# A TensorE loop over expert tiles, turned by two products

## What is computed

```python
router_logits = x @ gate_w.T
probs = jax.nn.softmax(router_logits, axis=-1)
topw, sel = jax.lax.top_k(probs, 2)
topw = topw / jnp.sum(topw, axis=-1, keepdims=True)
combine = jnp.sum(jax.nn.one_hot(sel, E) * topw[..., None], axis=1)
gu = jnp.einsum('th,efh->etf', x, gate_up_w)      # E = 8, F = 1024, H = 256
gate, up = gu[..., :F], gu[..., F:]
hact = up * jax.nn.gelu(gate, approximate=False)
expert_out = jnp.einsum('etf,ehf->eth', hact, down_w)
out = jnp.einsum('eth,te->th', expert_out, combine)
```

## Time and profile before

| what | value |
|---|---|
| median of three runs | 1316.13 us (1311.7 to 1317.1) |
| span of the profiled execution | 1255.6 us, 60.5 us under the median |
| TensorE (PE) busy | 1159.1 us, 92% of the span |
| DVE, ScalarE, GpSimd busy | 885.0, 570.0, 268.5 us |
| expert part, 338.47 to 931.90 us | 593.4 us, TensorE busy 567.8 |
| whole tiles, half tiles | 28, 11 |
| matmuls of line 1772, of line 1785 | 3744, 1608 |

### The profile page before, as it was taken

How to read it: one execution, slowest core, us unless ns; L and a number is a source line. 1 busy time by engine, 2 the same in 40 slices (tenths; PEclk the granted TensorE clock), 3 DMA queues, 4 the chain that set the end, 5 groups by cost and what they waited for, 6 DMA issues and landing times.

```text
span 1255.6 us, 35065 instructions
## 1 busy us (share of the span) xinstructions
PE 1159.1 (92%) x11816; PEld 968.8 (77%) x11816; DVE 885.0 (70%) x2697; ACT 570.0 (45%) x1187; POOL 268.5 (21%) x394
## 2 busy tenths in 40 slices
PE   4799999998699998999998999999998999999996
PEld 3678888886488887787887888888886777877774
DVE  4688888897376665757656666776566878778773
ACT  4466666675232422424224242422234666666553
POOL 6024444444310000000000000000014344444310
PEclk9899999998799999999999999999998999999998
DMA  9544444445341221222312222100023222322210
GB/s 282 209 131 153 147 149 152 152 142 179 132 157 45 73 96 41 86 63 64 98 39 80 74 67 88 41 31 31 27 65 95 72 78 82 93 88 77 79 39 17
DMA packets 82755, 119.67 MB, mean 95 GB/s; under 512 B 27325, under 2 KB 52557, under 8 KB 80588
## 3 DMA queue, kind: packets, MB, share of 16 engines
q1 hardware_dynamic: 64172, 60.32, 15.4%
q0 software_dynamic: 12848, 49.05, 11.7%
q10 hardware_dynamic: 5616, 8.78, 1.9%
HBM read 63.81 MB, written 47.58 MB: 89 GB/s over the span
## 4 chain that ended last, share of the span: by engine, by line
PE 77%; DVE 9%; issue 6%; ACT 3%; SPq 2%; ACTq 2%; DMA 1%; DVEq 0%; POOL 0%; POOLq 0%
PE bank L1772 27%; PE bank L1785 14%; PE bank L1599 7%; PE bank L1533 6%; PE bank L1455 5%; PE bank L1475 3%; PE bank L1516 3%; PE bank L1586 3%; PE bank L1518 2%; PE bank L1539 2%; PE bank L1597 1%; PE bank L1610 1%; PE bank L1501 1%; PE bank L1559 1%; DVE bm L1093 1%
## 5 line engine op out<-in xcount | busy, mean ns | idle before, releaser
L1772 PE MATMUL bank<-tiles,we 128*128 128x256 f16 (+1 forms) x3744 | 395.1, 259 | 5.8 <-issue 4.9
L1772 PEld LDWEIGHTS bank<-tiles,we 128*128 128x128 f16 x3744 | 325.9, 98 | 47.1 <-issue 13.3
L947 ACT ACTIVATE tiles<-bank 128x256 f32<-128x256 f32 (+1 forms) x312 | 109.5, 354 | 336.3 <-PE bank L1772 300.4
L1785 PE MATMUL bank<-we,tiles 128*128 128x256 f16 x1608 | 225.5, 274 | 20.7 <-DVE tiles L1385 19.8
L1381 DVE SCALAR_TENSOR_TENSOR tiles<-bank,tiles 128x256 f32<-128x256 f32 (+1 forms) x312 | 119.8, 384 | 164.7 <-ACT tiles L947 161.2
L1785 PEld LDWEIGHTS bank<-we,tiles 128*128 128x128 f16 x1608 | 148.1, 98 | 59.3 <-DVE tiles L1385 33.7
L1533 PE MATMUL bank<-qT,kbd 128*128 128x256 f16 x960 | 150.3, 274 | 2.7 <-issue 2.0
L1093 DVE TENSOR_REDUCE bm<-bank 128x4 bf16<-128x308 f32 x256 | 116.8, 474 | 28.1 <-PE bank L1518 19.9
L1387 DVE TENSOR_TENSOR tiles<-tiles 128x256 f16<-128x256 f32 (+1 forms) x312 | 121.1, 388 | 11.8 <-DVE tiles L1385 1.3
L471 DVE TENSOR_TENSOR pr<-pr 128x512 f16<-128x512 f32 x160 | 108.3, 681 | 25.2 <-ACT pr L809 21.5
L1533 PEld LDWEIGHTS bank<-qT,kbd 128*128 128x128 f16 x960 | 92.1, 98 | 19.6 <-issue 3.1
(11 more groups left out here) (198 smaller groups left out, 1654.0 us busy)
## 6 DMA issues: line engine op xcount, KB each, us to landing
expert_out<-zeros SPq DMA_DIRECT2D x16, 896.0 KB, 4.2
wes<-in_guT POOLq DMA_DIRECT2D x9, 1024.0 KB, 5.1
tiles<-expert_in SPq DMA_DIRECT2D x29, 256.0 KB, 2.6
pr<-in_guT POOLq DMA_DIRECT2D x7, 1024.0 KB
yg<-in_dnT POOLq DMA_DIRECT2D x7, 1024.0 KB
expert_out<-tiles ACTq DMA_DIRECT2D x28, 256.0 KB, 2.1
expert_in<-zeros POOLq DMA_DIRECT2D x8, 640.0 KB, 13.1
xin<-in_x SPq DMA_DIRECT2D x16, 256.0 KB, 2.8
```

What stands on the lines that cost most here:

```text
L947: act.activation(ge[:, fc % 2, 0:n * P], bank[1 + fc % 3][:, 0:n * P], ACT.Gelu, scale=INV).then_inc(s.gelu, 1)
L1772: last = pe.matmul(bank[1 + fc % 3][:, half * S:half * S + w * P], gate_up[:, par, c, i, col:col + P], xT[:, j, c, 0:w * P], start=n == 0, ...
L1785: last = pe.matmul(bank[4 + t][:, 0:D], act16[:, fc % 4, i, t * P:(t + 1) * P], we[:, par, 2, j, fc * D:(fc + 1) * D], start=fc == 0 and n ...
```

## The change

TensorE's stream in the expert part is changed, and one small DVE operation is added; ScalarE, GpSimd and SyncE keep their streams.

- Between two whole tiles of one expert TensorE now does down 6, up 0 of the next tile, down 7, up 1 of the next tile (`pass_on`). The loop over an expert's whole tiles holds products 2 to 7 of a tile and this passage, and takes in all whole tiles but the last; up 0 and up 1 of the first tile stand before it (`begin`), the last tile behind it (`middle`, `finish`).
- For that TensorE reads eight more bounds from the table (`final`, the last whole tile of each expert), which DVE writes with one operation more (whole tiles plus first tile minus 1).
- Up 0 takes its matmuls in another order: first the eight with the high half of x, gate and up, then the four with the low half. The wait for `tile_low` stands before these four. The gate and the up product share a bank, of which only the first matmul now opens the sum.

The first piece is TensorE before, from the second written-out tile of expert 0 into the loop. Line 1785 is down, line 1772 is up; the 18 are down 5, 6 and 7.

Behind that wait, down 7 now stands in TensorE's queue too. The diff:

```diff
--- before.py
+++ after.py
@@ -267,7 +267,7 @@
         slotx = sb("slotx", [P, NB * QT * 2], F32)
         slott = sb("slott", [P, NB * QT * 2], F32)
         slotz = sb("slotz", [P, NB * QT * 2], F32)
-        tbl = sb("tbl", [1, 4 * E + 1], I32)
+        tbl = sb("tbl", [1, 5 * E + 1], I32)
         nhf = sb("nhf", [P, E], F32)
         whole = sb("whole", [P, E], F32)
         hsf = sb("hsf", [P, E + 1], F32)
@@ -1306,7 +1306,7 @@
             place(at(0, 15))
 
 
-            ch = Chain(dve, s.count_step, 27, 0)
+            ch = Chain(dve, s.count_step, 28, 0)
             ch.link(dve.tensor_tensor(ntf[:], carry[:], cst[:, C_BASE:C_BASE + E], ALU.subtract))
             ch.link(dve.tensor_scalar(nti[:], ntf[:], float(P - 1), None, ALU.add))
             ch.link(dve.tensor_scalar(nti2[:], nti[:], 7, None, ALU.logical_shift_right))
@@ -1325,6 +1325,8 @@
             ch.link(dve.tensor_copy(tbl[0:1, 0:E + 1], tsf[0:1]))
             ch.link(dve.tensor_tensor(tbl[0:1, 2 * E + 1:3 * E + 1], tsf[0:1, 0:E], whole[0:1],
                                       ALU.add))
+            ch.link(dve.scalar_tensor_tensor(tbl[0:1, 4 * E + 1:5 * E + 1], tsf[0:1, 0:E], -1.0, whole[0:1],
+                                             ALU.add, ALU.add))
             ch.link(dve.tensor_scalar(tbl[0:1, 3 * E + 1:4 * E + 1], hsf[0:1, 0:E], float(P), None, ALU.mult))
             dve.tensor_copy(tbl[0:1, E + 1:2 * E + 1], carry[0:1, :]).then_inc(s.tiles_counted, 1)
 
@@ -1763,15 +1765,18 @@
             def up(par, g, fc, w=QT):
 
                 pe.wait_ge(s.product, g * FC + ((fc + 6) if fc >= 3 else (7, 8, 6)[fc]))
-                for half in range(2):
+                high = [(c, i, 0) for c in range(KC) for i in range(2)]
+                low = [(c, 0, 1) for c in range(KC)]
+                order = [(half, t) for half in range(2) for t in high + low]
+                if fc == 0:
+                    order = [(half, t) for terms in (high, low) for half in range(2) for t in terms]
+                for n, (half, (c, i, j)) in enumerate(order):
+                    if fc == 0 and n == 2 * len(high):
+                        pe.wait_ge(s.tile_low, g + 1)
                     col = half * F + fc * P
-                    high = [(c, i, 0) for c in range(KC) for i in range(2)]
-                    for n, (c, i, j) in enumerate(high + [(c, 0, 1) for c in range(KC)]):
-                        if fc == 0 and half == 0 and n == len(high):
-                            pe.wait_ge(s.tile_low, g + 1)
-                        last = pe.matmul(bank[1 + fc % 3][:, half * S:half * S + w * P],
-                                         gate_up[:, par, c, i, col:col + P], xT[:, j, c, 0:w * P],
-                                         start=n == 0, stop=n == 5)
+                    last = pe.matmul(bank[1 + fc % 3][:, half * S:half * S + w * P],
+                                     gate_up[:, par, c, i, col:col + P], xT[:, j, c, 0:w * P],
+                                     start=n == 0 or (fc > 0 and n == 6), stop=n in (5, 11) if fc else n == 11)
                 last.then_inc(s.gate_up, 1)
 
             def down(par, g, fc, w=QT):
@@ -1791,29 +1796,45 @@
                            for e in range(1, E + 1)]
             end = [pe.value_load(tbl[0:1, 2 * E + 1 + e:2 * E + 2 + e], min_val=1, max_val=TILES)
                    for e in range(E)]
-
-            def tile(e, g, w):
-                par = e % 2
+            final = [pe.value_load(tbl[0:1, 4 * E + 1 + e:4 * E + 2 + e], min_val=1, max_val=TILES)
+                     for e in range(E)]
+
+            def begin(e, g, w):
                 pe.wait_ge(s.expert_weights, e * 3 + 3)
                 pe.wait_ge(s.tile_high, g + 1)
-                up(par, g, 0, w)
-                up(par, g, 1, w)
+                up(e % 2, g, 0, w)
+                up(e % 2, g, 1, w)
+
+            def middle(e, g, w):
                 for fc in range(2, FC):
-                    up(par, g, fc, w)
+                    up(e % 2, g, fc, w)
                     if fc == 2:
                         t_x(g + 1)
-                    down(par, g, fc - 2, w)
-                down(par, g, FC - 2, w)
-                down(par, g, FC - 1, w)
+                    down(e % 2, g, fc - 2, w)
+
+            def finish(e, g, w):
+                down(e % 2, g, FC - 2, w)
+                down(e % 2, g, FC - 1, w)
+
+            def pass_on(e, g):
+                down(e % 2, g, FC - 2)
+                pe.wait_ge(s.tile_high, g + 2)
+                up(e % 2, g + 1, 0)
+                down(e % 2, g, FC - 1)
+                up(e % 2, g + 1, 1)
 
             t_x(0)
             for e in range(E):
-                tile(e, bound[e], QT)
-                tile(e, bound[e] + 1, QT)
-                with pe.Fori(bound[e] + 2, end[e]) as g:
-                    tile(e, g, QT)
+                begin(e, bound[e], QT)
+                with pe.Fori(bound[e], final[e]) as g:
+                    middle(e, g, QT)
+                    pass_on(e, g)
+                middle(e, final[e], QT)
+                finish(e, final[e], QT)
                 with pe.Fori(end[e], bound[e + 1]) as g:
-                    tile(e, g, 1)
+                    begin(e, g, 1)
+                    middle(e, g, 1)
+                    finish(e, g, 1)
 
             b1 = at(1, 0)
             for n in range(10):
```

## The result

| | before | after |
|---|---|---|
| median, same chip, 6 runs each | 1313.1 us (1309.5 to 1317.1) | 1324.6 us (1322.6 to 1327.3) |
| ratio after / before | | 1.0075 [1.0053, 1.0098] |
| expert part, first up to last down | 593.4 us | 600.4 us |
| 8 readings behind the first 16 | none | 5.2 us |

What follows compares the result with a forecast made beforehand. TensorE's expert matmuls, 41% of the span, were taken to bound the kernel. Readings 5.2, later down 7 3.3 and DVE's second tile 4.0 made +12.5 us on 1316.1: 1328 us, range 1320 to 1334.

Steps and rivals of the forecast that it cites:

- The base: Outside the profiled span: median 1316.1 us against a span of 1255.6, leaving 60.5 us that the change does not touch.
- The readings, +5.2: Before the first tile: TensorE's eight added table readings, 0.655 us each, lie uncovered on the path, +5.2 us.
- The low half: At 20 whole-tile boundaries: up 0's low matmuls wait 0.39 us for DVE's low half of x; 0.19 us more each.
- T: Moment at a boundary between whole tiles when down 7 starts in the kernel before, its activation having come from DVE's cast.
- Down 7 later, +3.3: At whole-tile boundaries: down 7 at T+1.50 delays ScalarE's copy and first gelu; down 0 waits 0.1 to 0.4 us, +3.3 us.
- DVE in the second tile, +4.0: In seven experts' second tiles: DVE, also making weight halves, cannot catch up, so T is 0.57 us late: +4.0 us.
- Jumps, 0: TensorE's whole-tile loop: 12 back jumps instead of 4, hidden under the instruction stream's 1.9 us lead; 0 us.
- The fourth rival: TensorE's loop: its 12 back jumps are not hidden, each costing 0.48 us again; 1330 us, chance 10%.
- Sum: Whole kernel: 5.2 + 3.3 + 4.0 = +12.5 us on the median 1316.1, given as 1328 us.
- The rivals on the far side: Whole-tile boundaries: two cases below the forecast where the low half comes in time; 1312.3 us (6%) and 1321 us (10%).
- the second one: Whole-tile boundaries: only the low half comes in time, down 0 still waits for ScalarE; 1321 us, chance 10%.
- the first one: Whole-tile boundaries: up 0 works as filler, low half in time, down 0 without wait; -3.8, 1312.3 us, chance 6%.

Runs made afterwards that it cites:

- the early gelu: Changed kernel, ScalarE making the second tile's first gelu before copying out the first tile's result: 1320.7 us, ratio 1.0030 to the kernel before.
- the early low half: Changed kernel, DVE making the next x's low half before the last subtraction in each expert's first two tiles: 1318.3 us, ratio 1.0021 to the kernel before.
- both helpers: Changed kernel with the early low half and the early gelu together: 1252.8 against 1254.8 us for the kernel before, ratio 0.9987.

## Why the prediction was right, and where not

The time was 1324.6 for a forecast of 1328, within the range, slower as said. The forecast's +12.5 stands beside +9.9 by the ratio and 12.2 by the profile. Of the 3.4 us between 1328 and 1324.6, 3.0 are the base: three more runs brought the median of before from 1316.1 to 1313.1. By steps:

- **The base.** "The profiled execution spans 1255.6 us; the median of the runs is 1316.1, and the 60.5 us around the span" was a wrong reading. Around the span of after lie 1.6 us (1326.1 less 1324.5). The profile of before was of an execution on a chip where the whole kernel is 60 us shorter; that chip's kind came up again with a median of 1254.8 us. The predicted span of 1268.1 is therefore meaningless, while the predicted difference was unhurt, since the expert part runs at full clock on both.
- **The readings, +5.2.** 394.31 - 389.16 = 5.15 us in the trace; +4.9 by the time when added alone. The Trainium skill's floor ("DMA: Bandwidth & Descriptors", Latency and other measured facts), some 600 ns, lies near the 0.655 us from one reading to the next; the reading by itself took 0.30 us (line 1799 above), half of that floor, and the rest of the 0.655 is its register operations.
- **The low half.** The low matmuls wait 0.38 us, from T+0.68 to T+1.06, on the seven boundaries of normal T; predicted 0.39. On eleven T is 0.57 us after down 6 instead of 0.20, and there they wait 0.76, to the same T+1.06, so that what follows T is the same, as the prediction said (the last two lie between). Down 7 at T+1.51 and up 1 at T+2.17, predicted 1.50 and 2.16.
- **Down 7 later, +3.3.** Copy at T+2.45 (2.48), first gelu at T+3.94 to T+4.26 (3.98 to 4.26), down 0 at T+5.26 to 5.32, 5.35 and 5.48 to 5.58 (5.30, 5.38, 5.58). Against before, boundary by boundary, that is 1.7 + 1.1 + 0.1 = 2.9.
- **DVE in the second tile, +4.0: the term that was too large.** The time line of the first expert's second tile: DVE's products follow each other by 1.73 us without idle, and the last (430.22) comes 11.08 us after down 0 (419.14), as worked out.

```profile
418.24 0.42 DVE L1383 SCALAR_TENSOR_TENSOR tiles<-bank,tiles 128x256 f32<-128x256 f32 x1 [3.42 <-ACT tiles L947]
418.79 0.29 DVE L1387 CAST tiles<-tiles 128x256 f16<-128x256 f32 x1
...
419.13 0.33 PEld L1790 LDWEIGHTS bank<-we,tiles 128*128 128x128 f16 x4 [0.17 <-DVE tiles L1387]
419.27 0.43 DVE L1389 TENSOR_TENSOR tiles<-tiles 128x256 f16<-128x256 f32 x1 [0.19 <-DVE tiles L1387]
...
419.61 0.42 DVE L1383 SCALAR_TENSOR_TENSOR tiles<-bank,tiles 128x256 f32<-128x256 f32 x1
...
426.77 0.42 DVE L1383 SCALAR_TENSOR_TENSOR tiles<-bank,tiles 128x256 f32<-128x256 f32 x1
...
428.50 0.42 DVE L1383 SCALAR_TENSOR_TENSOR tiles<-bank,tiles 128x256 f32<-128x256 f32 x1
...
430.22 0.42 DVE L1383 SCALAR_TENSOR_TENSOR tiles<-bank,tiles 128x256 f32<-128x256 f32 x1
```

  But only experts 0, 2 and 4 have 11.07 to 11.09; 1, 3, 5 and 6 have 10.93, and the last 10.55. That makes 3 x 0.56 + 4 x 0.41 = 3.3 us. In those four, product 1 follows product 0 by 1.22 us (496.61 to 497.83 in expert 1) instead of 1.37 (418.24 to 419.61), because the first subtraction follows its cast by 0.33 us instead of 0.48; all steps behind it are the same. They are the experts in whose first tile T is late, in both kernels; why the subtraction waits less there is not known. The 1.37 of the earlier trace rows was that of expert 0. I had read one expert and multiplied by seven.
- **Jumps, 0.** The branch (count, ns min/median/max, first and last start) runs under the lead of TensorE's stream; 12 of the 20 jump back, and between up 1 and up 2 there is no gap on any of the 20 boundaries. The fourth rival is out.

```profile
L1829 PEldq COMPARE_BRANCH  x20: 67/209/231, 415.4 to 961.6; - x20
```

- **Sum.** 5.2 + 2.9 + 3.3 = 11.4, and 0.8 that no term had: the first tiles of experts 2 and 4, behind ScalarE's table load, are 1.3 us longer from down 0 to T and down 0 of the very first tile follows its up 0 0.8 us sooner; the rest are tenths in single tiles. The two errors of size, -0.4 and -0.7, and these 0.8 nearly cancel, which is luck. The ratio's 7.0 to 12.9 us holds the sum. In all kernels that keep the 16 readings or more at the head, the measured middle lies 1 to 4 us under what its profile adds up to (12.2 and 9.9 here, 7.7 and 3.9 with the early gelu), which no run explains.
- **A sign that misleads.** The prediction named whole tiles shorter than 16.54 us as a sign that it was wrong. Five first tiles are, 16.06 to 16.34 from up 0 to up 0 (experts 1, 3, 5, 6 and 7), but only because the next up 0 now stands ahead of down 7; the second tiles take 16.62 to 17.01. From down 0 to down 0 no whole tile with another behind it is shorter than before by more than 0.03 us.

The rivals on the far side were tried as kernels: the early low half gives the second one's down 0, and both helpers make the first one's filler. Its condition was put as the low half's arrival by T+0.67; the helper brought it to T+0.60, and the wait went on the boundaries of normal T. Where T is late, the eight high matmuls end at T+0.30, and 0.3 us of the wait stay.

## What to carry to other kernels

Work moved in front of an instruction as a filler waits for its own inputs first: ask which engine makes them, and whether it makes them before or after the thing that was waited for. Here the filler's input came a microsecond after the result it was to bridge, and two small moves on the producing engines (the input first, the next activation before the copy out) turned the expert part's +7 us into -4.5. Loop bounds read from memory cost 0.655 us each where the engine has nothing queued; taken to places where it waits anyway or has work queued, they left the expert part within the spread of its profiles (594.6 us); and a profile's span should be set against a run's time of the same chip before anything is said to lie "around" it.

## What the runs showed of the hardware

- The same program takes 1255 us on some chips and 1315 on others. Nearly all of the difference lies in block 0's attention, with a granted clock of 1.00 against 0.85; the expert part's clock is 0.99 on both. What makes the chips differ is not shown.
- Behind an idle of 5.2 us TensorE's granted clock was 0.50 (1.2 GHz) for 2.7 us. The wait's price was a quarter more than its length.
- ScalarE stood for 2.5 us at the back jump of a loop whose body is two experts, while TensorE's 20 branches over one tile's body, 12 of them jumping back, show no stop (0.07 to 0.23 us each, hidden).
